# Graph layers fed by indirect gathers: GpSimd's gathers paced in pairs through SyncE, and SyncE's loads moved to ScalarE

## What is computed

```python
# layer 0: message of an edge, summed by destination, then the node's own product
all_feat = concatenate([x[dst], x[src], edge_attr, u_per_node[dst]], axis=-1)
msg = relu(all_feat @ W1 + b1)
agg = segment_sum(msg, dst)
x = layernorm(x + relu(concatenate([x, agg, u_per_node], -1) @ W2 + b2))
# layer 1: attention over the incoming edges, one matrix per edge type
Z = einsum('ni,rio->nro', x, fc_weight)
z_s, z_d = Z[src, etype], Z[dst, etype]
e = relu(sum(concatenate([z_s, z_d], 1) * attn_weight[etype], 1))
ex = exp(e - segment_max(e, dst)[dst])
x = layernorm(x + segment_sum((ex / segment_sum(ex, dst)[dst])[:, None] * z_s, dst))
```

## Time and profile before

| | |
|---|---|
| three runs | 5622.56, 5624.8, 5631.35 us |
| the profiled execution | 5585.7 us, its span 5584.0 us |
| busy, share of the span | PE 55%, PE weight load 50%, DVE 53%, ACT 23%, POOL 54% |
| mean granted TensorE clock | 0.519 |
| gathers | 1563 in each layer; their queue moved 105 MB in 100032 packets |
| moved in the whole kernel | 300 MB, mean 54 GB/s |

### The profile page before, as it was taken

How to read it: one execution, slowest core, us unless ns; L and a number is a source line. 1 busy time by engine, 2 the same in 40 slices (tenths; PEclk the granted TensorE clock), 3 DMA queues, 4 the chain that set the end, 5 groups by cost and what they waited for, 6 DMA issues and landing times. The chain is left out here.

```text
span 5584.0 us, 71029 instructions
## 1 busy us (share of the span) xinstructions
PE 3080.6 (55%) x17849; PEld 2768.8 (50%) x17849; DVE 2980.1 (53%) x9486; ACT 1278.0 (23%) x4180; POOL 3034.1 (54%) x3265
## 2 busy tenths in 40 slices
PE   2265555455555555545784066555555656655576
PEld 1264444444444444444772055555555555555565
DVE  1265554455555555555773065555555555555567
ACT  0100000000000000000022044444444444444455
POOL 5525555555555555555215706666666666666631
PEclk5555555555555555555566555555555555555555
DMA  3211111111111111111125101111111111111111
GB/s 115 82 45 51 46 53 53 45 51 46 54 52 45 52 46 53 52 44 52 53 100 181 28 27 46 47 47 47 47 47 47 47 47 47 47 47 47 47 38 32
DMA packets 172540, 300.15 MB, mean 54 GB/s; under 512 B 71719, under 2 KB 78235, under 8 KB 158844
## 3 DMA queue, kind: packets, MB, share of 16 engines
q0 software_dynamic: 100032, 105.03, 9.8%
q1 hardware_dynamic: 70662, 188.25, 9.4%
q10 hardware_dynamic: 1462, 2.30, 0.1%
HBM read 260.36 MB, written 34.99 MB: 53 GB/s over the span
## 5 line engine op out<-in xcount | busy, mean ns | idle before, releaser
L453 POOL DMA_INDIRECT ring<-Btab,idx x1563 | 1486.5, 951 | 1214.7 <-DVE XA L846 610.3
L453 POOL DMA_INDIRECT ring<-Ztab,idx x1563 | 1479.9, 947 | 922.2 <-issue 400.0
L719 PE MATMUL p_m<-A,oht 128*128 x1664 | 438.3, 365 | 1061.8 <-DVE full L853 1023.5
L1344 PE MATMUL p_s<-ring,ohx 128*128 x3328 | 808.9, 420 | 191.2 <-issue 187.2
L732 PE MATMUL p_s<-msg,oh 128*128 128x64 f32 x3328 | 763.8, 418 | 178.2 <-issue 137.0
L1344 PEld LDWEIGHTS p_s<-ring,ohx 128*128 128x128 f32 x3328 | 738.8, 325 | 214.4 <-issue 214.1
L732 PEld LDWEIGHTS p_s<-msg,oh 128*128 128x128 f32 x3328 | 731.0, 329 | 204.8 <-issue 204.5
L873 DVE TENSOR_REDUCE p_t<-p_m 128x256 f32<-128x768 f32 x416 | 380.0, 958 | 817.4 <-remote 809.6
L719 PEld LDWEIGHTS p_m<-A,oht 128*128 128x128 bf16 x1664 | 237.6, 145 | 1153.8 <-issue 1109.8
L1402 DVE TENSOR_REDUCE mslot<-p_x 128x8 f32<-128x1024 f32 x208 | 254.7, 1225 | 896.8 <-remote 882.6
L632 ACT ACTIVATE msg<-p_t 128x512 f32<-128x512 f32 x208 | 124.2, 597 | 2552.7 <-issue 2161.9
(11 more groups left out here) (211 smaller groups left out, 2716.4 us busy)
## 6 DMA issues: line engine op xcount, KB each, us to landing
drow<-drow_d SPq DMA_DIRECT2D x104, 1024.0 KB
eaT<-in_eaT_in SPq DMA_DIRECT2D x208, 128.0 KB
Ztab<-Z_stage SPq DMA_DIRECT2D x49, 536.0 KB, 5.1
ring<-Btab,idx POOLq DMA_INDIRECT x1563
ring<-Ztab,idx POOLq DMA_INDIRECT x1563
xTB<-in_xTB_in SPq DMA_DIRECT2D x7, 448.0 KB, 4.0
Btab<-B_stage SPq DMA_DIRECT2D x7, 448.0 KB, 6.0
ring<-in_xTA_in SPq DMA_DIRECT2D x7, 448.0 KB, 4.2
```

Source lines behind the costliest of these rows:

```text
L453: e.indirect_dma_start(out=ring[:, place(t), :], out_offset=None, in_=table[:, :], in_offset=bass.IndirectOffsetOnAxis(ap=idx[:, t:t + 1], ...
L719: e.matmul(parts(j), OHT[:, s % 2, j, :], A.A3[:, bass.ds(b, 1), :].rearrange("p a c -> p (a c)"), start=True, stop=True)
L1344: last = e.matmul(pS[s % 2][h][:, j % 4, :], OHx[:, s % 2, j, :], ring[:, bass.ds(t, 1), 0:D + 1], start=True, stop=True)
```

## The change

POOL's gathers: in both layers each odd gather (j = 1, 3, 5, 7) from number `first` on is followed by an increment of `ping`. SP does nothing in the loops but `echoes`: for each ping it makes four increments of `echo`, the first of them in the instruction that waits for the ping. Each odd gather but the first such one waits until `echo` stands at four times the number of pings before it. `first` is 80 in layer 0 and 0 in layer 1.

SP's loads of the loops are now issued by ACT, in both copies of layer 0's loop: the attributes of step s + 1 between the relu of step s - 1 and that of step s, the row loads and x ahead of them; in layer 1 the row load of group g + 2 ahead of the scaled one-hots of the last step of group g (SP issues the first two). Two counts that nobody waits for, `oh` in layer 0 and `act` in layer 1, are gone.

```diff
@@ gathers, and a new function before it
+ECHO = 4
+
+def echoes(e, ping, echo, first):
+    for n in range(len(range(first + 1, NT, 2))):
+        e.wait_ge(ping, n + 1).then_inc(echo, 1)
+        for k in range(ECHO - 1):
+            e.sem_inc(echo, 1)
+
-def gathers(e, A, ring, table, idx, s_g, landed, used, summed, free={}):
+def gathers(e, A, ring, table, idx, s_g, landed, used, summed, ping, echo, first, free={}):
...
         if s >= RT and j in (2, 4, 6):
             e.wait_ge(summed, O * (s - RT + BEHIND - 1) + j)
+        if j % 2 and t > first + 1:
+            e.wait_ge(echo, ECHO * ((t - first) // 2))
         e.indirect_dma_start(out=ring[:, place(t), :], out_offset=None, in_=table[:, :],
                              in_offset=bass.IndirectOffsetOnAxis(ap=idx[:, t:t + 1], axis=0)).then_inc(s_g[s % len(s_g)], 16)
+        if j % 2 and t >= first:
+            e.sem_inc(ping, 1)
         if s and j == min(3, NT - s * O - 1):
             counted(s - 1)
@@ phase_layer0
+    EARLY = 10 * O
...
         @block.sync
-            treg = e.alloc_register("l0st")
...
             rows_loaded(e, A, drow, s_dr, S["oht"], 0)
-            def loads(of):
-                for s in range(SO):
-                    if s == 4:
-                        e.wait_ge(T["zero"], 1)
-                        e.dma_start(A.x1, A.x_in.rearrange("(b p) d -> p b d", p=P)).then_inc(A.s_x, 16)
-                    if s % G == 0 and s + G < SO:
-                        rows_loaded(e, A, drow, s_dr, S["oht"], s // G + 1)
-                    e.reg_load(treg, xrow[0:1, s, 0:1])
-                    if s >= QE:
-                        e.wait_ge(S["c"], s - QE + 1)
-                    t = e.snap(treg, min_val=1, max_val=TO)
-                    e.dma_start(eaT[0:2 * DE, s % QE, :, :], of[bass.ds(t, 1), :, :, :].rearrange("a f i k -> (a f) i k")).then_inc(s_ea[s % QE], 16)
-            bad = descends(e, A, "l0_sp")
-            with e.If(bad == 0):
-                loads(A.eaT_in)
-            with e.Else():
-                loads(A.eaT_s)
+            echoes(e, S["ping"], S["echo"], EARLY)
...
         @block.scalar
             e.wait_ge(T["typd"], 32)
+            e.wait_ge(T["table"], 64)
             e.activation(A.acc0, A.ones[:, 0:D].unsqueeze(1).to_broadcast([P, NB + 1, D]), ACT.Copy, scale=0.0).then_inc(T["zero"], 1)
-            for s in range(SO):
-                e.wait_ge(S["pre"], s + 1)
-                e.activation(msg[:, s % 2, :, :], pT[:, :, :], ACT.Relu).then_inc(S["msg"], 1)
+            treg = e.alloc_register("l0at")
+            def attributes(s, of):
+                e.reg_load(treg, xrow[0:1, s, 0:1])
+                if s >= QE:
+                    e.wait_ge(S["c"], s - QE + 1)
+                t = e.snap(treg, min_val=1, max_val=TO)
+                e.dma_start(eaT[0:2 * DE, s % QE, :, :], of[bass.ds(t, 1), :, :, :].rearrange("a f i k -> (a f) i k")).then_inc(s_ea[s % QE], 16)
+            def relus(of):
+                for s in range(QE):
+                    attributes(s, of)
+                for s in range(SO):
+                    if s == 4:
+                        e.wait_ge(T["zero"], 1)
+                        e.dma_start(A.x1, A.x_in.rearrange("(b p) d -> p b d", p=P)).then_inc(A.s_x, 16)
+                    if s % G == 0 and s + G < SO:
+                        rows_loaded(e, A, drow, s_dr, S["oht"], s // G + 1)
+                    if s and s + QE - 1 < SO:
+                        attributes(s + QE - 1, of)
+                    e.wait_ge(S["pre"], s + 1)
+                    e.activation(msg[:, s % 2, :, :], pT[:, :, :], ACT.Relu).then_inc(S["msg"], 1)
+            bad = descends(e, A, "l0_act")
+            with e.If(bad == 0):
+                relus(A.eaT_in)
+            with e.Else():
+                relus(A.eaT_s)
...
@@ phase_layer1
         @block.sync
-            for g in range(SO // G):
+            for g in range(2):
                 rows_loaded(e, A, drow, s_dr, S["oht"], g)
+            echoes(e, S["ping"], S["echo"], 0)
...
             for s in range(SO + 2):
+                if s % G == G - 1 and s // G + 2 < SO // G:
+                    rows_loaded(e, A, drow, s_dr, S["oht"], s // G + 2)
                 if s < SO:
                     scored(s)
```

More of the change, by code:

```diff
@@ L519, in phase_layer0 @@
         A3v = A.A3[:, 0:NB, :].rearrange("p (q h) c -> p q h c", h=2)
-        names = "oht oh c m0 m1 full pre msg s acc landed".split()
+        names = "oht c m0 m1 full pre msg s acc landed ping echo".split()
         S = {n: sem("l0_" + n) for n in names}
@@ L550, in _ @@
             rows_loaded(e, A, drow, s_dr, S["oht"], 0)
-            def loads(of):
-                for s in range(SO):
-                    if s == 4:
-                        e.wait_ge(T["zero"], 1)
-                        e.dma_start(A.x1, A.x_in.rearrange("(b p) d -> p b d", p=P)).then_inc(A.s_x, 16)
-                    if s % G == 0 and s + G < SO:
-                        rows_loaded(e, A, drow, s_dr, S["oht"], s // G + 1)
-                    e.reg_load(treg, xrow[0:1, s, 0:1])
-                    if s >= QE:
-                        e.wait_ge(S["c"], s - QE + 1)
-                    t = e.snap(treg, min_val=1, max_val=TO)
-                    e.dma_start(eaT[0:2 * DE, s % QE, :, :], of[bass.ds(t, 1), :, :, :].rearrange("a f i k -> (a f) i k")).then_inc(s_ea[s % QE], 16)
-            bad = descends(e, A, "l0_sp")
-            with e.If(bad == 0):
-                loads(A.eaT_in)
-            with e.Else():
-                loads(A.eaT_s)
+            echoes(e, S["ping"], S["echo"], EARLY)
         @block.gpsimd
         def _(e):
-            gathers(e, A, ring, A.Btab, idx, s_g, S["landed"], S["full"], S["acc"], {XT0 // O: (T["a"], len(CHUNKS))})
+            gathers(e, A, ring, A.Btab, idx, s_g, S["landed"], S["full"], S["acc"], S["ping"], S["echo"], EARLY, {XT0 // O: (T["a"], len(CHUNKS))})
         @block.scalar
@@ L831, in onehots @@
                                 in1=A.dstl[:, s * O:(s + 1) * O].unsqueeze(2).to_broadcast([P, O, P]),
-                                op=ALU.is_equal).then_inc(S["oh"], 1)
+                                op=ALU.is_equal)
                 e.wait_ge(s_dr[s // G % 2], 16 * (s // G // 2 + 1))
@@ L1261, in phase_layer1 @@
         pB = [pair[1][:, 512 - 3 * O:512].rearrange("p (j c) -> p j c", c=3) for pair in p_s]
-        names = "oht e ev ohe x m3 b ed ohx s0 s acc dve act ex ty landed".split()
+        names = "oht e ev ohe x m3 b ed ohx s0 s acc dve ex ty landed ping echo".split()
         S = {n: sem("l1_" + n) for n in names}
@@ L1270, in _ @@
         def _(e):
-            for g in range(SO // G):
+            for g in range(2):
                 rows_loaded(e, A, drow, s_dr, S["oht"], g)
+            echoes(e, S["ping"], S["echo"], 0)
         @block.gpsimd
         def _(e):
-            gathers(e, A, ring, A.Ztab, idx, s_g, S["landed"], S["s"], S["acc"])
+            gathers(e, A, ring, A.Ztab, idx, s_g, S["landed"], S["s"], S["acc"], S["ping"], S["echo"], 0)
         @block.scalar
@@ L1283, in weights @@
                 e.activation(ex[:, o, :], ed[:, o, :], ACT.Exp).then_inc(S["ex"], 1)
-                e.activation(ff[:, r, :], fd[:, r, :], ACT.Exp).then_inc(S["act"], 1)
+                e.activation(ff[:, r, :], fd[:, r, :], ACT.Exp)
                 e.wait_ge(S["ex"], s + 1)
```

## The result

The change makes the kernel 1% slower: 5682.9 us (four runs, 5672.5 to 5692.0) against 5627.2 us (four runs), ratio 1.0099, 95% interval 1.0076 to 1.0121. The profiled execution after has a span of 5687.7 us. The forecast was 5128; the time is inside the range, on the wrong side of no change. The trace of before behind the rows (5584.0 us) is some 40 us shorter than the timing runs of before, so where that matters a second trace of the same kernel at 5624.8 us is set beside it.

What follows compares the result with a forecast made beforehand. Bound: POOL's gathers hold PE, and PE's lateness stops POOL. Profiled 5586 - 1380 (relief) + 883 (exposed waits) = 5089 us, plus 39 to the runs' median, gave 5128; the range took in the floor, 4245, and reached up to 5900.

Steps and rivals of the forecast that it cites:

- The bound: Both layers' loops: gathers hold PE, PE's lateness stops POOL, the stop frees PE; POOL idles 988.8 and 725.5 us.
- What it can be worth: Both layers, if PE were never held and POOL alone set the end: together 1380 us saved.
- The floor of 4206 us: Whole kernel with PE never held: 5585.7 - 1380 = 4206 us on the profiled execution's scale.
- these 1380 us: Savings of 681 and 135 us in layer 0, 438 and 126 in layer 1, before and after the last gathers.
- The wait: POOL's wait at every second gather: about 1523 pairs at 0.58 us, 883 us added.
- I take 0.58, wholly exposed: Each pair's trip POOL, SP, POOL paid in full at POOL's wait; bounds 0 and 1.30 us.
- The trip's price: POOL to SP and back: two hand-overs, 0.52 us, plus three further increments, 0.06 together; 0.58 us.
- Hidden: Rival at POOL's wait: the 0.58 us answer fits under the 1.25 us gather, PE stays held, 5625 us; chance 0.18.
- The sum: Whole kernel: 5586 - 1380 + 883 = 5089 us, plus 39 to the runs' median, 5128 us.
- The moved loads: Loads issued by ACT instead of SP, covered by ACT's idle time before relus and exponentials: cost 0.
- The first attribute load behind the zeroing: Start of ACT's queue: behind 5.48 us of zeroing, first step up to 6 us later; cost 0, at most 6.
- A step of POOL's: POOL's gathers for one step: 8 x (0.95 + 0.30) = 10.0 us, longer than PE's steps of 7 to 8 us.

Runs made afterwards that it cites:

- second set: Runs where the kernel of before takes 5627.1 us; the change as it stands, repeated against that kernel: 5680.5 us, ratio 1.0087.
- loads alone: The changed kernel without pings, answers and POOL's wait, loads still moved, against the kernel of before (5585.7 us): 5603.3 us, ratio 1.0032.
- the unheld run's row above: SP's answers with sixteen for each ping in place of four, against the kernel of before at 4193.2 us: 4190.2 us, ratio 0.9992.

## Why the prediction was wrong

**The bound: right.** Beside runs of gathers PE is late, and the lateness stops POOL. By the Trainium skill, "SBUF — State Buffer", "Who interferes with whom", PE never waits on anyone and a DMA never contends with a compute engine; the trace agrees with that where 969 products stand beside 185 gathers, and doesn't where 128 do, though no run shows that PE's memory port is what is held. Which one it is depends on where the kernel runs, and no row of one profile tells it.

**What it can be worth: right, in part by luck.** The floor of 4206 us is what the kernel takes where nobody is held, 4193 us. Both stretches of gathers came out as worked out (1853 and 1954 us). But there the setup before gather 80 takes 137 us and not 169, which the forecast had left as it was, and the end after the last gather of layer 1 takes 85 and not 69; the two misses partly cancel. The change brought none of these 1380 us: the pauses that were to bring them never showed in its steady parts.

**The wait: this step failed.** "I take 0.58, wholly exposed" should have been 0. The trip's price in the open was not far off: 0.22 us from ping to last answer with four answers, and 0.26 us from the last answer to the gather where POOL does wait (32 answers), 0.48 together. What was wrong is the exposure. The gather that asks for the answer is due two gathers, 2.5 us, after the gather that its ping belongs to, and the ping doesn't wait for that gather either. POOL's pings after a pause, in the trace of after (L469 is the line of the ping):

```profile
L469 POOLq EVENT_SEMAPHORE  x4: 17/17/17, 1446.9 to 1449.9; - x4
```

Four pings leave within 3.0 us, 1.0 us apart, and the gathers that stand before them in the program start at 1448.33, 1450.83, 1453.33 and 1455.82, 1.5 to 5.9 us later. Over a whole trace of the change (second set) the ping is a median of 4.1 us ahead of its gather. So the cover is some 6 us and not the 1.25 of the rival, and it hides far more than the mean trip of the held runs, 1.77 to 1.98 us: the last answer to the ping of 1457.79 came 7.2 us later, at 1464.97, and the gather that asks for it starts at 1465.81 after the same 0.30 us. Only where the answers hold POOL's queue up each time does the lead go: with 32 the ping leaves 0.22 us before its gather (1455.76 for the gather of 1455.98), the cover is down to 2.5 us, and the pause shows. The argument "PE is released only where POOL truly pauses, so I can't book the relief without paying for pauses" was sound; what followed from it is that a hidden wait gives no relief, and that was the rival *Hidden*, which had the better row for it (1.25 us of cover) and got 0.18. Its marks are there: gaps of 0.30, a pattern of long and short steps (17.5 and 10.2 in place of 20.2 and 6.9), DVE's long waits. The page "Perfetto Trace Analysis", section "DMA Instruction — SWDGE (GPSIMD)", of the Trainium skill had a gather leave the queue before it executes; the pings ahead of their gathers agree.

**The sum was right for another kernel.** With sixteen answers a pair takes 3.09 us in layer 0 and 3.12 in layer 1 (forecast 3.08), layer 0 saves 245 us net before its last gather (forecast 681 - 430 = 251) and 134 behind it (135), and layer 1 loses 47 and saves 109 (forecast 453 - 438 = 15 lost, 126 saved). The time is 5146 at a level where before takes 5586, so the forecast to hold it against is the 5089 before the 39 us were added: 57 us off, not 18. That a mean gap of 0.89 us (0.93 in layer 1) meets the forecast's 0.88 is luck. The forecast had four answers at 0.58 us a trip, always exposed; here it is sixteen, 3.29 us a trip, with pauses near 2 us before some odd gathers and none before others. That an exposed wait is paid in full shows with 32: the pair is 3.57 us, and the relief no longer pays for it.

**The moved loads: 0 was wrong by one row.** In the steady part it is 0, as worked out. But the row loads were priced as one kind at 0.47 us; the one behind x's load takes 10.01 us to issue, the cover of 6.29 us isn't enough, and the stage with it is 13 us longer. The first attribute load behind the zeroing costs nothing that can be seen (first relu at 184.5 before and 184.4 with the loads alone).

**The sign of the remainder.** *Hidden* had no price for a hidden update. Between loads alone and the change lie 26 us (5599.9 to 5626.2 in the traces), with 55 lost in layer 0's steady part. That the earlier hold comes of the pings and answers is what the pair of runs shows; whether it is their number or the wait in POOL's queue stays open, since the kernel without the wait, and the one with one answer, were never measured where PE is held.

**Smaller readings.** A step of POOL's was put at 8 gathers, 10.0 us; 1563 gathers over 208 steps are 7.5, and unheld steps of layer 0 come every 9.2 to 9.4 us. PE's clock is 0.50 in the first two stretches of the earlier trace rows and 0.52 in the third. The 2.52 us of the earlier trace rows are the idle time; the two products start 2.78 us apart. None of them enters the sum.

## What to carry to other kernels

A pacing wait does something only if the answer outlasts the work between question and wait: work out that cover first, with the lead that the asking queue has over its engine, and look in the profile whether the gap has grown. If it hasn't, what is left is the cost of its updates. When issues move to an engine that computes, price each by what stands before it in the same queue, not by its kind. And before tuning against a stall that shows in one place, run the kernel in another: sixteen answers gain 8% in the one held place where they ran and neither gain nor lose (0.9992, 0.9983 to 1.0002) where it isn't. A mix, sixteen in layer 0 and fewer in layer 1, whose steady part got 120 us slower with sixteen, wasn't run.

## What the runs showed of the hardware

The same kernel has three levels: 4193 us in four sets, 5586 and 5627 in one each (the runs of the result are at 5627 too), each steady within 0.4%; within a set all kernels were held or none was. One chip number shows up with both 4193 and 5627. The trace that the prediction read (5585.7) was of the second level and the runs beside it of the third, which is the 39 us between them. The trace of after is of the third level too. What sets the level wasn't found. The clock is the same (0.51 to 0.52), and so are the gathers.

The hold isn't PE's alone. Of SP's answers, 0.017 us in the median, 1542 of 6088 take over 0.3 us where before takes 5627, and 1367 where it takes 5586, most of them near 0.70; of the 22830 in the unheld run's row above none takes over 0.26. The same row for the change in the second set:

```profile
L443 SPq EVENT_SEMAPHORE  x4566: 2/17/1422, 168.4 to 5480.2; - x199
```

Nor is it only the passing of counts. The sixteen instructions of PE that sum one step's messages wait for nothing between the first and the last, and only the last raises a count. In the trace of before, in a held stretch, they stand apart:

```profile
224.01 0.27 PE L732 MATMUL p_s<-msg,oh 128*128 128x64 f32 x1
226.79 0.26 PE L732 MATMUL p_s<-msg,oh 128*128 128x64 f32 x1 [2.52 <-issue]
229.59 0.26 PE L732 MATMUL p_s<-msg,oh 128*128 128x64 f32 x1 [2.54 <-issue]
```

Of 3120 such neighbours in layer 0, 81 start over 1 us apart there, 297 in the trace of before at 5625, 288 to 355 with the change, and none in three unheld traces or in the held ones with sixteen and 32 answers. So what is held beside the gathers are instructions of PE that touch no count as well as increments of SP's; by what path stays open. An engine that increments a semaphore at a steady pace shows the hold directly.
